# First LoRA products of a fused LoRA and mixture-of-experts FFN kernel: from one quarter of the partitions to four

## The reference, cut to what matters

```python
hidden_i  = x @ wi.T                                                # 256 -> 1024
hidden_i += 2 * (x @ common_wi_a.T) @ common_wi_b.T                 # rank 16, shared
hidden_i += 2 * (x @ experts_wi_a[id].T) @ experts_wi_b[id].T       # rank 16, of the sequence's expert
hidden_o  = relu(hidden_i) @ wo.T   (+ the same two corrections with wo_a, wo_b)
# mixture of experts on h = hidden_o
probs = softmax(mean_over_tokens(h) @ gate_w); the two largest, scaled to sum 1
out = x + sum_k p_k * (gelu(h @ w1[e_k] + b1[e_k]) @ w2[e_k] + b2[e_k])
```

## Time and profile before

| | before |
|---|---|
| median of three runs | 266.29 us |
| the profiled execution's own time | 265.94 us |
| its span, first to last instruction | 264.2 us |
| PE busy | 260.0 us (98%) |
| DVE / ACT / POOL busy | 174.3 / 174.8 / 160.7 us |
| mean granted PE clock | 0.999 of full |

### The profile page before, as it was taken

How to read it: one execution, slowest core, us unless ns; L and a number is a source line. 1 busy time by engine, 2 the same in 40 slices (tenths; PEclk the granted TensorE clock), 3 DMA queues, 4 the chain that set the end, 5 groups by cost and what they waited for, 6 DMA issues and landing times.

```text
span 264.2 us, 3622 instructions
## 1 busy us (share of the span) xinstructions
PE 260.0 (98%) x1156; PEld 212.8 (81%) x1156; DVE 174.3 (66%) x284; ACT 174.8 (66%) x279; POOL 160.7 (61%) x192
## 2 busy tenths in 40 slices
PE   8999999999999999999999999999999999999995
PEld 4778888888878888888888888888888888888884
DVE  1882867376998636657594866658856567665665
ACT  3857365455466289888976887676777677774650
POOL 2267997933398977897549999456366366331100
PEclk9999999999999999999999999999999999999999
DMA  6987120201032102211202112203202206000004
GB/s 187 382 322 244 35 79 0 84 1 40 0 124 79 51 28 80 82 22 59 83 0 63 60 38 79 79 0 83 79 2 79 78 4 200 0 0 2 0 1 159
DMA packets 11139, 19.76 MB, mean 75 GB/s; under 512 B 2000, under 2 KB 2256, under 8 KB 10992
## 3 DMA queue, kind: packets, MB, share of 16 engines
q1 hardware_dynamic: 10544, 18.61, 21.5%
q10 hardware_dynamic: 576, 0.92, 1.0%
HBM read 17.43 MB, written 2.10 MB: 74 GB/s over the span
## 4 chain that ended last, share of the span: by engine, by line
PE 98%; DVE 0%; issue 0%
PE out_ps L762 16%; PE out_ps L759 16%; PE out_ps L758 16%; PE hid_ps L758 15%; PE hid_ps L759 14%; PE hid_ps L762 14%; PE hid_ps L959 2%; PE hid_ps L798 1%; PE out_ps L888 1%; PE hid_ps L802 1%; PE hid_ps L806 1%; PE hid_ps L910 1%; PE hid_ps L900 1%; DVE x_sb L1271 0%; DVE y_sb L1159 0%
## 5 line engine op out<-in xcount | busy, mean ns | idle before, releaser
L413 POOL TENSOR_TENSOR up_lo<-up_raw,up_hi 128x512 fp32r<-128x512 f32 x41 | 53.0, 1311 | 37.1 <-ACT up_hi L573 36.9
L758 PE MATMUL out_ps<-hid_hi,down_hi 128*128 128x512 f32 x190 | 74.0, 390 | 0.0
L762 PE MATMUL out_ps<-hid_hi,down_lo 128*128 128x512 f32 x190 | 74.0, 389 | 0.0
L759 PE MATMUL out_ps<-hid_lo,down_hi 128*128 128x512 f32 x190 | 74.0, 389 | 0.0
L758 PE MATMUL hid_ps<-act_hi,up_hi 128*128 128x512 f32 x166 | 64.9, 391 | 0.0
L759 PE MATMUL hid_ps<-act_lo,up_hi 128*128 128x512 f32 x166 | 64.7, 390 | 0.0
L762 PE MATMUL hid_ps<-act_hi,up_lo 128*128 128x512 f32 x166 | 64.6, 389 | 0.0
L605 ACT ACTIVATE hid_ps<-hid_ps,bias_sb 128x512 f32<-128x512 f32 x64 | 42.2, 659 | 29.1 <-DVE hid_ps L1080 18.0
L1054 DVE SCALAR_TENSOR_TENSOR hid_lo<-hid_ps,mix,hid_hi 128x512 fp32r<-128x512 f32 x64 | 47.9, 748 | 20.3 <-ACT hid_hi L619 19.7
L419 POOL TENSOR_TENSOR down_lo<-down_raw,down_hi 128x512 fp32r<-128x512 f32 x24 | 32.4, 1349 | 37.2 <-ACT down_hi L583 37.2
L619 ACT ACTIVATE hid_hi<-hid_ps,mix 128x512 fp32r<-128x512 f32 x64 | 44.1, 690 | 4.7
(11 more groups left out here) (98 smaller groups left out, 241.9 us busy)
## 6 DMA issues: line engine op xcount, KB each, us to landing
up_raw<-in_w SPq DMA_DIRECT2D x16, 256.0 KB, 2.8
down_raw<-in_w SPq DMA_DIRECT2D x16, 256.0 KB, 2.6
lora_raw<-in_lora SPq DMA_DIRECT2D x10, 256.0 KB, 4.8
down_raw<-in_woT SPq DMA_DIRECT2D x8, 256.0 KB, 3.8
up_raw<-in_wiT SPq DMA_DIRECT2D x7, 256.0 KB, 4.2
outT<-x_sb SPq DMA_DIRECT2D x6, 256.0 KB, 3.5
x_sb<-in_x1T SPq DMA_DIRECT2D x1, 1024.0 KB, 7.6
x_sb<-in_x0bT SPq DMA_DIRECT2D x1, 512.0 KB, 4.0
```

The costliest lines, as they stand in the source:

```text
L413: ins = eng.tensor_tensor(up_lo[:, n, cols], up_raw[:, n, cols], f32(up_hi[:, n, cols]), ALU.subtract)
L758: eng.matmul(out, w_h, a_h, start=start, stop=False, skip_group_check=onto)
L759: eng.matmul(out, w_h, a_l, start=False, stop=False, skip_group_check=onto)
L762: return eng.matmul(out, w_l, a_h, start=False, stop=stop, skip_group_check=onto)
```

## The change

Four products of two matmuls each (up of set 0, up of set 1, down of set 0 and up of set 2) are now made from float32 rows. The tile `lora_first` becomes 128 partitions by two groups by 384 columns. A group holds four pairs of blocks, one on each quarter of 32 partitions, and is loaded by one DMA of its own. `first_raw_factors` makes four matmuls from group 0, each on its own quarter and to its own `out_ps` bank; `second_raw_factors` makes four from group 1, behind set 0's up tiles. So `down_factor(0)` and the product for `up(2)` from `lora_st` are gone.

Further:

- the first merge and the first high copy are cut in three pieces, of 128, 128 and 256 columns in place of two of 256;
- set 0's up tiles are written in another order (`first_half`, `second_half`), with f (the half of the features) outermost at the very start;
- of lots 0 to 3 of sequence 0 only one block of 256 columns is copied and split (`parts`);
- SP loads the lots later, behind the second group, down 0 and up 2, and the first expert number is read without bounds;
- the product for `down(1)` moves from ahead of the third up tile of set 1 to behind it; its merge on DVE moves behind `hid_low(1, 1)`;
- on ACT and POOL several lot copies, `raw_high` and `token_sum` change places within sets 0 to 2.

```diff
-    UP_FACTOR_AT = {0: [1], 1: [2], 2: [3, 4], 3: [5], 5: [6], 6: [7]}
+    UP_FACTOR_AT = {2: [3, 4], 3: [5], 5: [6], 6: [7]}
+    PRODUCTS = [("u", 1), ("d", 0), ("u", 2)]
-        lora_first = sb("lora_first", [G, LOT + SW])
+        lora_first = sb("lora_first", [P, 2, P + SW])
+        def parts(b, lot):
+            if b == 0 and lot < 4:
+                return [0] if lot < 2 else [1]
+            return [0, 1]
+        FIRST_COLS = [slice(0, P), slice(P, SW), slice(SW, 2 * SW)]
 # SP
-            e = number(ids[0:1, 0:1])
-            eng.dma_start(lora_first[:, :], early[bass.ds(e, 1), :, :].rearrange("e r c -> (e r) c"))\
-               .then_inc(s_lora_first, 16)
+            def load_first(n, e):
+                eng.dma_start(lora_first[:, n, :], early[bass.ds(e, 1), n, :, :].rearrange("e r c -> (e r) c"))\
+                   .then_inc(s_lora_first[n], 16)
+            e = eng.value_load(ids[0:1, 0:1])
+            load_first(0, e)
             load_x0(eng, 1)
             eng.dma_start(x_sb[:, 0, 1, :, :], x0bT[:, :, :]).then_inc(s_x0b, 16)
             load_up(eng, 1)
+            load_first(1, e)
+            next_down(0)
+            next_up(2)
             load_lora(0, 1, e)
-            load_lora(0, 0, e)
-            next_down(0)
-            load_lora(0, 3, e)
-            next_up(2)
             load_lora(0, 2, e)
             next_down(1)
+            load_lora(0, 0, e)
+            load_lora(0, 3, e)
 # PE
+            def first_one(t, f, kd, low_w, low_a, start=False, stop=False):
+                w, a = (up_lo if low_w else up_hi), (act_lo if low_a else act_hi)
+                return eng.matmul(hid_ps[:, 2 * t + f, :], w[:, 0, block(kd * 2 + f)], a[:, 0, kd * NT + t, :],
+                                  start=start, stop=stop)
+            def raw_factor(n, rows, bank):
+                return eng.matmul(out_ps[:, bank, 0:SW], lora_first[block(rows, G), n, 0:P],
+                                  lora_first[block(rows, G), n, P:P + SW], start=True, stop=True)
+            def first_raw_factors():
+                eng.wait_ge(s_lora_first[0], 16)
+                raw_factor(0, 0, 0)
+                raw_factor(0, 1, 1).then_inc(s_prod0, 1)
+                raw_factor(0, 2, 2)
+                raw_factor(0, 3, 3).then_inc(s_prod, 1)
+            def second_raw_factors():
+                eng.wait_ge(s_lora_first[1], 16)
+                eng.wait_ge(s_merge0, len(FIRST_COLS))
+                eng.wait_ge(s_merge, product_count("u", 1))
+                raw_factor(1, 0, 2)
+                raw_factor(1, 1, 3).then_inc(s_prod, 1)
+                raw_factor(1, 2, 0)
+                raw_factor(1, 3, 1).then_inc(s_prod, 1)
             warm_up(WARM_UP)
-            raw_up_factor(0, out_ps[:, 0, 0:SW], out_ps[:, 1, 0:SW])
-            raw_up_factor(1, out_ps[:, 2, 0:SW], out_ps[:, 2, SW:2 * SW])
-            first_pair(0)
-            first_pair(1)
-            down_factor(0, out_ps[:, 3, :])
+            first_raw_factors()
+            first_half()
+            second_half()
+            second_raw_factors()
 # PE, set 1
-                        next_up_factor(q)
                     down(q - 1, 1)
-                    next_down_factor(q)
+                    if q > 1:
+                        next_down_factor(q)
                     plain_tile(q, 2)
+                    if q == 1:
+                        next_down_factor(q)
 # DVE
             merge0(0)
             merge0(1)
+            merge0(2)
             up0_low(0)
+            x0_low(eng, 1, 0)
             up0_low(1)
-            x0_low(eng, 1, 0)
             x0_low(eng, 0, 1)
-            merge_up(1, out_ps[:, 2, :])
             x0_low(eng, 1, 1)
-            lora_low(0, 1)
+            merge_up(1, out_ps[:, 2:4, 0:SW])
             hid_low(0, 0)
             hid_low(0, 1)
-            merge_down(0, out_ps[:, 3, :])
+            merge_down(0, out_ps[:, 2:4, 0:SW])
+            merge_up(2, out_ps[:, 0:2, 0:SW])
             hid_low(0, 2)
             hid_low(0, 3)
-            lora_low(0, 3)
+            lora_low(0, 1)
```

More of the change, by code:

```diff
@@ L86, in build @@
                 "m7": (S3, T3)}
[L91 to L93 removed]
+    UP_FACTOR_AT = {2: [3, 4], 3: [5], 5: [6], 6: [7]}
+    PRODUCTS = [("u", 1), ("d", 0), ("u", 2)]
+    for n in range(1, N_COND):
         ups = [("u", to) for to in UP_FACTOR_AT.get(n, ())]
@@ L184, in build @@
         s_x0b, s_x1 = sem("s_x0b"), sem("s_x1")
-        s_lora_first = sem("s_lora_first")
+        s_lora_first = [sem(f"s_lora_first{n}") for n in range(2)]
         s_up_raw = [sem(f"s_up_raw{n}") for n in range(NU)]
@@ L311, in load_lora @@
                 if b:
-                    eng.wait_ge(s_llo[0][lot], 2)
+                    eng.wait_ge(s_llo[0][lot], len(parts(0, lot)))
                 cols = block(lot, LOT)
@@ L442, in lora_low @@
                 eng.wait_ge(s_lhi, LORA_HI.index((b, lot)) + 1)
-                for n in range(2):
+                for made, n in enumerate(parts(b, lot)):
                     lora_lo(eng, b, lot, n)
-                    eng.wait_ge(s_llo[b][lot], n + 1)
+                    eng.wait_ge(s_llo[b][lot], made + 1)
             def logit_terms(b):
@@ L553, in lora_high @@
             def lora_high(b, lot):
+                made = parts(b, lot)
+                to = slice(lot_at(b, lot) + made[0] * SW, lot_at(b, lot) + (made[-1] + 1) * SW)
+                raw = slice(lot * LOT + made[0] * SW, lot * LOT + (made[-1] + 1) * SW)
                 eng.wait_ge(s_lora[b][lot], 16)
@@ L556, in lora_high, with up0_high @@
                     eng.wait_ge(s_prod, product_count("d", lot - 1))
[L557 to L562, removed]
+                eng.activation(lora_st[:, to], lora_raw[0:LR, raw], ACT.Copy).then_inc(s_lhi, 1)
+            def up0_high(n):
+                eng.wait_ge(s_merge0, n + 1)
+                cols = FIRST_COLS[n]
                 eng.activation(up_hi[:, 0, cols], up_raw[:, 0, cols], ACT.Copy).then_inc(s_up0hi, 1)
@@ L800, in first_pair @@
                     for f in range(2):
[L801 to L808, removed]
+                        first_one(1, f, kd, True, False)
@@ L810, in plain_tile @@
+                for kd in range(KD):
+                    eng.wait_ge(s_x0lo[kd][1], 1)
+                    for f in range(2):
+                        ins = first_one(1, f, kd, False, True, stop=(kd == KD - 1))
+                        if kd == KD - 1:
+                            ins.then_inc(s_up, 1)
             def plain_tile(q, j):
@@ L896, in up_factor @@
                 for lot in lots_of("u", q):
-                    eng.wait_ge(s_llo[b][lot], 2)
+                    eng.wait_ge(s_llo[b][lot], len(parts(b, lot)))
                 for kd in range(KD):
```

125 lines of the change are left out of this document (85 added, 40 removed).

## The result

The changed kernel takes 267.57 us (median of eight runs, 267.23 to 268.21), the kernel before 266.49 us in the same sessions (265.86 to 267.18). The ratio is 1.0044, interval 1.0025 to 1.0063: 1.1 us slower, inside "no change" by the bound of 0.5%, and inside the range, 0.8 us above the forecast of 266.8 and 0.4 us under the range's upper end. (The ratio is not the quotient of the two medians; it comes with its own interval.) The sum in the prediction, +0.57, was made of wrong terms, though, and the largest part of what was measured has no term in it at all.

A forecast was written before the change was run, and what follows sets the result against it. The prediction took PE, busy 260.0 of 264.2 us, as the bound. Its terms -0.24 + 0.10 - 0.75 + 1.46 = +0.57 gave 266.5 against the profiled execution, 266.8 against the median; range 265.6 to 268.0 us.

The forecast's parts named there:

- Start of set 0: First up matmul 0.13 us earlier through narrower first pieces, and set 0's up matmuls 0.11 us shorter: -0.24 us.
- half overlap: Float32 products: a product's first pass runs beside the second pass of the one before; eight passes start over 0.87; chance 0.45.
- Every input ready by at least 0.1 us: In set 0's new order no up matmul waits for its inputs, so up to 0.11 us is gained.
- Load of the first rows: First DMA brings 192 KB for 96, issued earlier but landing later: cost 0 to 0.4 us, taken as +0.1.
- Products and wait removed: Pair ahead of set 1 gone, 0.23 us, and a later pair with its 0.29 wait, 0.52: together -0.75 us.
- Products added: Second group ahead of set 1: switch in 0.41, passes 0.87, switch out 0.41, less one matmul's 0.23: +1.46 us.
- full overlap: Rival: all quarters run beside each other, second group +0.81, instructions -0.29 in all, 266.0 us; chance 0.20.
- The holes: Switching PE between 128-row and 32-row matmuls costs 0.41 to 0.42 us start to start, about 0.2 extra each.
- Wait in set 1: Rival: DVE's merge of down 1 comes late for the fourth up tile, +0.6 us, 267.4; chance 0.10.
- clock: Rival: PE's idle 0.5 us between products and set 0 brings back the low clock, +1.6 us, 268.4; chance 0.05.
- Whatever moves set 1's start should move the end by as much: From set 1 to the end PE has no slack behind it, so a shift there reaches the end in full.

The follow-up runs named there:

- again_before: The kernel before, unchanged, run once more for a second profile: 266.73 us, ratio 1.0001.
- one_quarter: The changed kernel with all eight float32 matmuls taken from partitions 0 to 31, so the output is not the reference's: 269.48 us, ratio 1.0093.
- two_pieces: The changed kernel with the first merge and first high copy in two pieces of 256 columns, as before: 267.48 us, ratio 1.0025.
- again_after: The changed kernel, unchanged, run once more for a second profile: 267.61 us, ratio 1.0038.
- pad_four_again: The changed kernel with `early` padded from 3 to 4.75 MB, the second run of that kernel: 266.60 us, ratio 1.0000.
- warm_nine: The changed kernel with 9 warm-up matmuls in place of 12: 267.50 us, ratio 1.0045.
- pad_four_mb: The changed kernel with `early` padded from 3 to 4.75 MB, 4 MB more than before has it: 266.82 us, ratio 0.9998.
- after_three_mb: The changed kernel with `early` padded to 3.75 MB, 3 MB more than before has it: 266.37 us, ratio 0.9993.
- before_large_early: The kernel before with only its input `early` enlarged in HBM from 0.8 to 3.1 MB, the same rows read: 268.03 us, ratio 1.0050.

## Why the prediction was right, and where it was wrong

The time fell inside the range and on the side of the sum, but by chance: the instructions' part came out 0.6 to 0.8 us lower than the sum had it (by the three runs of the changed kernel with the fast tail), and a term of 1.2 us was missing. By its own steps:

- **Start of set 0, -0.24.** The mechanism was right. From the load to the first up matmul it went from 2.03 to 1.69, -0.34, more than the half overlap allowed for: the merge started 0.83 us after the load, where before it was 0.82, so the second matmul cost nothing. Against again_before, whose warm-up ended at the low pace like the changed kernel's, it is 0.52 (2.21 to 1.69), as before's own products are slower there. Set 0's own matmuls went from 5.32 to 5.26 us, -0.06 where I had -0.11. one_quarter and two_pieces show the two parts. "Every input ready by at least 0.1 us" was wrong in two of the changed kernel's profiles: PE stood 0.2 us (again_after) and 0.4 us (pad_four_again) for the second half of x.
- **Load of the first rows, +0.10.** Not shown by any run. Issue came at 2.63 to 2.88 in the nine profiles of the changed kernel and its variants, against 2.95 to 3.03 in the five of before: 0.1 to 0.4 us earlier, as taken. The rows landed 2.4 to 3.2 us after the issue, at 5.24 to 5.83, where those of before landed at 4.95 to 5.23. But in all 13 profiles with 12 warm-up matmuls the load stands behind the last of them, 0.30 to 0.32 us after its start, or 0.56 to 0.57 where it ran at the low pace: 4.92 to 5.23 in before, 5.77 to 6.08 in again_after, whose rows had landed at 5.24. So there it was the warm-up that set the load. Only in warm_nine did the rows decide (landing 5.44, load 5.50). An execution of the changed kernel with a warm-up as early as before's, where late rows would cost something, was not profiled.
- **Products and wait removed, -0.75.** Right. Line 974 follows with no idle time ahead, and set 1 runs 0.227 from start to start.
- **Products added, +1.46.** This is the step that failed. The trace has 1.07 from start to start, less one 0.227: +0.84, the bound of full overlap (0.81) and not the middle. I had argued that the two passes of a product (here one matmul) follow each other in the list, so that only neighbours could overlap. The rows show four first passes together and then four second ones. Whether the passes stand so in PE's list, or PE pulls them together, the trace does not tell; my assumption on their order was wrong in its effect. The rival "full overlap", given 0.20, was the case, and its -0.29 for the instructions alone (ratio 0.9989) lies inside the intervals of pad_four_mb, pad_four_again and after_three_mb (0.9998, 1.0000 and 0.9993); no difference at all lies inside them too, so it is the trace that shows the overlap, not these times. The Trainium skill's figure for a packed group (TensorE: Matmul & The Clock Gate, Measured speedup vs the span model), one matmul's time, holds here: two passes, 0.32 us from the load to the second pass, for one matmul or for four.
- **The holes.** Right: 0.32 to the next load, seen at both switches of the second group. The hole into the first group is one as well, and not the landing of the rows that I had left open for the earlier trace rows: again_after has 0.31 there with the rows landed 0.8 us before. The hole out of the first group lies under the wait for the merge. Without holes, 0.4 us less by the prediction's own reading, the second group would have gained 0.3 against the 0.75 that it replaces; with them it gives nothing.
- **Wait in set 1, clock.** Neither came. The pause of 0.9 us before set 0 did not bring back the low level: the up matmuls behind it start 0.23 apart.
- **The missing term.** "Whatever moves set 1's start should move the end by as much" was wrong about the very end. In the profile pair that was first compared, the last DVE instruction moved by +0.82 (of which +1.19 is warm-up and -0.37 the change), and the end by +2.0. The stores' tail, +1.2 us, follows for the most part from `early` having grown by 2.25 MB, a line of host code that I read as part of the load alone. before_large_early shows that the size alone brings 1.0 us (2.42 to 3.42 on the same chip), pad_four_mb that the instructions alone do not bring it. The other 0.25 us goes with the changed kernel's own timing of the first two stores, which two_pieces has as before and with it the shorter tail.

What stays open: how the size of one input slows the stores. What fits the runs is where the output lies in HBM (the host code allocates it behind the inputs, and with `early` last among them the tail was the same). That is argued, not shown: no run here shows an address, and the output was not moved by itself.

No version beats before beyond its interval. after_three_mb, the changed kernel on whole megabytes, has the lowest median, 266.37 us, and its interval reaches to 1.0005.

## What to carry to other kernels

Cut the span before comparing: up to the first real work, from there to the last compute instruction, and the tail of the stores. Here the three moved by up to +1.2, by -0.4 and by +1.2 us. The first was the pace of the warm-up, the middle one was the change, and the last was four fifths the size of an array. When a change alters the size of any array in HBM, run the old kernel with the new sizes first. And when products are packed beside each other, count the switches of the array's mode as well as the passes.

## What the runs showed of the hardware

- Four float32 matmuls (32 rows, 256 columns) on four quarters take two pass steps together, 0.32 us from the first weight load to the second passes; on one quarter their eight passes take 1.92 us (one_quarter).
- Each switch between 32-row and 128-row matmuls keeps the next weight load back until 0.30 to 0.32 us after the last matmul's start; from start to start that is 0.41 to 0.42 us by the working in the prediction, where two starts without a switch are 0.23 us apart. The 96-row matmuls of line 974 have no such hole: the matmul behind them starts 0.12 us after the second of them.
- The last stores (1 MB in five) end 2.4 to 2.7 or 3.4 to 3.7 us after the last compute instruction. What decides is the size of an input that they do not touch, at 0, 2, 3, 4 against 2.25 MB more; with several stores in flight the rate in the slow case is some 180 to 260 GB/s, in the fast one 257 to 380.
- The warm-up matmuls, 0.43 us apart at first (1.2 GHz), went over to 0.22 (2.4 GHz) after different times from one execution to the next; so the first product's load lies between 5.2 and 6.4 us. Four profiled executions with the instructions of before and the fast tail bear the link out: 265.94 and 265.99 us with the load at 5.23 and 5.32, 267.31 and 267.51 with it at 6.42. The spread of 0.9 to 1.6 us that most kernels here have is of that size, but for executions without a profile the link is argued.
- The granted clock reads 1.00 from 1 to 5 us in the changed kernel's profile, where its warm-up matmuls start 0.43 us apart, the spacing of the lower level.
